# Layer 3 attention: where the first two score products of the next group and the value projections stand on TensorE

## The reference, cut to what matters

```
x = x + L3_xattn(layernorm(x), ctx_1024, mask, W_Q, b_Q, W_K, b_K, W_V, b_V, W_O, b_O)

def L3_xattn(q_input, kv_input, key_padding_mask, ...):      # 16 heads of 8
    q, k, v = q_input @ W_Q + b_Q, kv_input @ W_K + b_K, kv_input @ W_V + b_V
    sim  = einsum('bhqd,bhkd->bhqk', q, k) / sqrt(8)
    sim  = where(mask, neg_inf, sim)
    attn = softmax(sim, axis=-1)
    out  = einsum('bhqk,bhkd->bhqd', attn, v)
    return out @ W_O + b_O
```

## Time and profile before

| | |
|---|---|
| median of 3 runs | 1711.19 us (1710.92 to 1711.9) |
| the profiled execution | 1711.91 us, its span 1709.8 us |
| PE / DVE / ACT busy | 1485.5 / 1249.9 / 841.4 us |
| granted TensorE clock, mean | 0.941 |
| layer 3 attention, first score product to last values product | about 1149 to 1557 us of the span |

### The profile page before, as it was taken

How to read it: one execution, slowest core, us unless ns; L and a number is a source line. 1 busy time by engine, 2 the same in 40 slices (tenths; PEclk the granted TensorE clock), 3 DMA queues, 4 the chain that set the end, 5 groups by cost and what they waited for, 6 DMA issues and landing times. The chain is left out here.

```text
span 1709.8 us, 39665 instructions
## 1 busy us (share of the span) xinstructions
PE 1485.5 (87%) x15230; PEld 1254.1 (73%) x15230; DVE 1249.9 (73%) x2582; ACT 841.4 (49%) x1265; POOL 332.0 (19%) x447
## 2 busy tenths in 40 slices
PE   3897387447899999999999999859999999996995
PEld 2897255236799999999999998426777777774895
DVE  4312664794888888888888886548888888884688
ACT  1342133233666666666666664325656656652432
POOL 0110000001333333333333330030111111100320
PEclk9899699668999999999999999979999999998998
DMA  1455067100211111111111100045455456441010
GB/s 36 112 171 122 20 162 167 37 1 6 67 37 37 37 36 36 36 42 53 46 39 36 36 0 5 2 106 122 118 129 138 111 123 145 116 89 51 26 37 23
DMA packets 93581, 115.95 MB, mean 68 GB/s; under 512 B 12712, under 2 KB 78808, under 8 KB 93464
## 3 DMA queue, kind: packets, MB, share of 16 engines
q1 hardware_dynamic: 93464, 114.25, 26.2%
HBM read 76.42 MB, written 0.46 MB: 45 GB/s over the span
## 5 line engine op out<-in xcount | busy, mean ns | idle before, releaser
L2365 DVE TENSOR_REDUCE l3att_parts<-PS 112x1 f32<-112x500 f32 x384 | 245.5, 668 | 55.8 <-PE PS L2104 48.1
L1643 ACT CAST l2att_PT<-PS 125x512 fp32r<-125x512 f32 x336 | 175.3, 594 | 221.1 <-PE PS L1582 221.1
L1683 DVE TENSOR_REDUCE l2att_neg<-PS 128x1 f32<-128x1500 f32 x112 | 192.7, 1720 | 77.0 <-PE PS L1575 77.0
L1689 DVE TENSOR_TENSOR l2att_PT<-PS,l2att_PT 125x512 fp32r<-125x512 f32 x336 | 210.1, 681 | 1.5 <-ACT l2att_PT L1643 1.5
L2231 ACT ACTIVATE l3att_P<-PS 125x1344 f32<-125x1344 f32 x128 | 165.3, 1292 | 76.9 <-PE PS L2123 76.9
L1582 PEld LDWEIGHTS PS<-all_ident,l_P 128*125 128x125 f32 x1344 | 163.6, 187 | 14.9 <-DVE l_P L1697 6.3
L1652 ACT ACTIVATE l_P<-PS,l2att_neg 128x1500 f32<-128x1500 f32 x112 | 171.3, 1529 | 3.9 <-DVE l2att_neg L1683 3.9
L1614 PE MATMUL PS<-l2att_PT,l_cc 125*128 125x256 f32 x576 | 170.5, 296 | 0.0
L1582 PE MATMUL PS<-all_ident,l_P 128*125 128x128 f32 x1344 | 165.4, 273 | 4.8 <-DVE l_P L1697 4.8
L2104 PE MATMUL PS<-l3att_KS,l3att_QB 97*112 97x500 f32 x384 | 155.8, 459 | 11.1 <-POOL l3att_QB L2291 4.9
L1616 PE MATMUL PS<-l2att_PT,l_cc 125*128 125x256 f32 x576 | 162.5, 282 | 0.0
(11 more groups left out here) (546 smaller groups left out, 2861.3 us busy)
## 6 DMA issues: line engine op xcount, KB each, us to landing
l3att_KS<-l3att_kh SPq DMA_DIRECT2D x128, 187.5 KB, 4.2
l_cT<-in_ctxT SPq DMA_DIRECT2D x18, 750.0 KB, 6.7
l_c<-in_ctx SPq DMA_DIRECT2D x16, 750.0 KB
l3att_cT<-in_ctxT SPq DMA_DIRECT2D x16, 750.0 KB, 4.4
l3att_KS<-l3att_kl SPq DMA_DIRECT2D x64, 187.5 KB, 4.4
l_QP<-in_ctx SPq DMA_DIRECT2D x10, 672.0 KB
l_QP<-in_ctxT SPq DMA_DIRECT2D x8, 750.0 KB, 7.2
l0f_w<-in_L_ffn_W SPq DMA_DIRECT2D x16, 256.0 KB, 3.0
```

What stands on the lines that cost most here:

```text
L1643: act.copy(PT[:, 4 * g:4 * g + 4, PLACE[u1], 0, :], PS[0:CHUNK, 3 * s1 + g, :].rearrange("k (c r) -> k c r", r=128)).then_inc(hi_in, 1)
L1683: v.tensor_reduce(neg[:, s:s + 1], E, XY_AXES, ALU.max, negate=True).then_inc(top_in, 1)
L1689: v.tensor_tensor(PT[:, 4 * g:4 * g + 4, at, 1, :], PS[0:CHUNK, 3 * s1 + g, :].rearrange("k (c r) -> k c r", r=128), PT[:, 4 * g:4 * g + 4 ...
L2365: v.tensor_reduce(parts[:, u % 2, half, i:i + 1], PS[0:HROWS, PLACES[p], 0:BANK_KEYS], X_AXIS, ALU.max, negate=True).then_inc(top_in, 1)
```

## The change

All the changes are in the order of work inside a step of the layer 3 attention. No instruction is added, removed or changed in shape.

- On TensorE `rows((0, 1))` of group n+1 now stands in step n, after the products with the values and ahead of `turned(1)`. `rows` takes the group's number for that.
- `project_values` moves from between score products 2 and 3 to behind the products with the values. Its wait on `p_in` is now for `powers(0)` of the same step, and the wait for ScalarE's copy of bank 5 moves from `turned(0)` to `turned(1)`.
- On ScalarE `values_out` moves from ahead of `powers(0)` to behind `outputs`.

```diff
--- before.py
+++ after.py
@@ -2078,24 +2078,24 @@
                     late = g == 1 and (known is None or SETS < known < GROUPS)
                     weighs = g == SETS - 1 and live(known, 2 * SETS - 1, GROUPS)
 
-                    def rows(places):
-
-                        s = u // SETS
+                    def rows(n, places):
+
+                        s, g = n // SETS % 2, n % SETS
                         for p in places:
                             half, i = p // BANKS, p % BANKS
                             if p == 0:
                                 pe.wait_ge(ks_in[s][g], n // UNROLL * 48 + 48)
                                 if g == 0:
                                     pe.wait_ge(mask_in[s], n // UNROLL * 16 + 16)
-                                if known == 0:
+                                if n == 0:
                                     pe.wait_ge(ones_in, 64)
                                 pe.wait_ge(qb_in, n + 1)
-                                if known != 0:
+                                if n > 0:
                                     pe.wait_ge(top_in, 6 * n - 1)
                             elif 2 <= p <= 4:
                                 pe.wait_ge(top_in, 6 * n + p - 1)
                             elif p == 5:
-                                if known is None or known >= 1:
+                                if n >= 1:
                                     pe.wait_ge(top_in, 6 * n)
                                 if g < BANKS and more:
                                     pe.wait_ge(kl_in, b * BANKS + BANKS + g + 1)
@@ -2114,7 +2114,7 @@
                         if known is None or known - 1 + part > 0:
                             pe.wait_ge(p_in, 2 * n - 2 + part)
                         for k in range(PART):
-                            if k == 4 and part == 0:
+                            if k == 4 and part == 1:
                                 if late:
                                     pe.wait_ge(vh_in, b * BANKS + BANKS)
                                 if g >= 2 and more:
@@ -2151,8 +2151,8 @@
                         mm.then_inc(o_ps, 1)
 
                     now, then, before = live(known, 0, GROUPS), live(known, 1, GROUPS), live(known, 2, GROUPS)
-                    if now:
-                        rows((0, 1))
+                    if n == 0:
+                        rows(0, (0, 1))
                     if then:
                         maxima()
                     if g < BANKS and more:
@@ -2165,22 +2165,22 @@
                                   OC[:, bass.ds((n - SETS) // SETS, 1), :, :].rearrange("p b g q -> p (b g q)"),
                                   start=True, stop=True).then_inc(den_ps, 1)
                     if now:
-                        rows((2,))
+                        rows(n, (2, 3))
+                    if then:
+                        turned(0)
+                    if now:
+                        rows(n, (4, 5))
+                    if before:
+                        values()
                     if late or g >= 2 and more:
-                        if known is None or known >= 2:
-                            pe.wait_ge(p_in, 2 * n - 2)
+                        if n >= 1:
+                            pe.wait_ge(p_in, 2 * n - 1)
                         if late:
                             project_values(pe, u // SETS, 2, 5)
                         else:
                             project_values(pe, 1 - u // SETS, g - 2, 5)
-                    if now:
-                        rows((3,))
-                    if then:
-                        turned(0)
-                    if now:
-                        rows((4, 5))
-                    if before:
-                        values()
+                    if n + 1 < GROUPS:
+                        rows(n + 1, (0, 1))
                     if then:
                         turned(1)
 
@@ -2248,14 +2248,14 @@
                             act.wait_ge(inv_in, (n - SETS) // SETS * 2)
                         act.copy(den[:, :, :].rearrange("p g q -> p (g q)"), PS[:, SIDE, 0:SET_ROWS]
                                  ).then_inc(den_in, 1)
+                    if live(known, 1, GROUPS):
+                        powers(0)
+                    if live(known, 2, GROUPS):
+                        outputs()
                     if g >= 2 and more:
                         values_out(act, b + 1, 1 - u // SETS, g - 2, 5)
                     if g == 1 and (known is None or SETS < known < GROUPS):
                         values_out(act, b, u // SETS, 2, 5)
-                    if live(known, 1, GROUPS):
-                        powers(0)
-                    if live(known, 2, GROUPS):
-                        outputs()
                     if live(known, 1, GROUPS):
                         powers(1)
 
```

## The result

The changed kernel takes 1725.74 us in the median of 4 runs (1723.33 to 1729.49), the kernel before in the same comparison 1711.06 us (4 runs, 1710.34 to 1711.9). The ratio is 1.0081, with a 95% interval of 1.0067 to 1.0095: slower by 0.8%. The profiled execution took 1725.39 us with a span of 1723.3 us, 13.5 us more than the span before.

A forecast was written before the change was run, and what follows sets the result against it. Bound: TensorE near its limit, in a ring of waits between three engines. +9.5 us for 14 batch entries, -0.7 twice in the last, +0.4 in the first: +8.5, 1720.4 profiled, median 1719.7; range 1705 to 1728, own 1714 to 1725.

The forecast's parts named there:

- the signs named for it: TensorE stalls for kl (0.4 to 0.5 us, three steps of four), waits for the exponential in all four, no copy wait.
- The kl ring: Step with g of 2: kh behind the exponential, then kl ending at 2.85, then product 5 at 3.00; 0.48 us lost.
- the term of +0.48: Step with g of 2: product 5 could start at 2.52 but waits for kl until 3.00 us.
- The copy's wait: Inside the transposed scores: the old 0.28 us wait for ScalarE's copy of the value projection goes.
- VectorE's bound in the step with g of 0: The next pair needs maximum 4's bank, so it starts at 4.83 and the step takes 5.93 us.
- the pair and the last half: Step with g of 2: next group's pair 5.65 to 6.10, then second half of transposed scores 0.65, ending at 6.75 us.
- The restart that I put on the value projection: A slow first product after the values, 0.10 us, making the value projection 0.97; charged in three steps.
- The rival with free restarts: Restarts cost nothing where work simply queues: +2.9 us, 1714.1 us, no measurable change; chance 0.10.
- the last batch entry: No keys or kl: two steps of 5.23 against 5.57 give -0.7 us, the last step, lacking the pair, another -0.7.
- kl is no limit: Rival: kh and kl done by 2.37, steps 1 to 3 at 6.20: 24.53 per batch entry, 1702.8 us; chance 0.12.
- VectorE alone sets the pace: Rival: VectorE's idle time is filled, 22.5 us per batch entry, 36 us less, 1675 us; chance 0.03.
- both unknown costs at their bad ends: Rival: kh after a gap (+6 us) and transposed scores with a restart (+5.6), up to 1731 us; chance 0.12.

The follow-up runs named there:

- after_kl_free: Changed kernel with product 5 waiting only for kh and kl computed from kh, so the result is incomplete: 1714.27 us, 1.0015 of the kernel before.
- after_values_first: Changed kernel, complete, with score product 5 moved behind the products with the values: 1711.41 us, 0.9998 of the kernel before.
- after_short_exp: Changed kernel with each step's second exponential reading two of its three banks, from the third step on: 1713.92 us, 1.0014 of the kernel before.
- proj_alone: Kernel before with only the value projections and their copies moved behind the products with values, pair unmoved: 1752.51 us, 1.0233 of the kernel before.
- gap4: Kernel before with score product 4 issued inside the transposed scores, before their fifth product: 1701.02 us, 0.9932 of the kernel before.
- gap4_g0: Kernel before with score product 4 inside the transposed scores and the early pair only for groups with g of 0: 1701.66 us, 0.9941.
- g0_early: Kernel before with the next group's pair early only where that group has g of 0: 1712.05 us, 1.0001 of the kernel before.
- pair_alone: Kernel before with only score products 0 and 1 of the next group moved early, value projections unmoved: 1728.56 us, 1.0092 of the kernel before.

## Why the prediction was right, and where it was short

The direction and the mechanism were right, and so were the signs named for it, with one reservation: the wait for the exponential is marked in one step of four, and in the others only the starts show it. In size the forecast was well short: 8.6 us were forecast (1711.06 to 1719.7) and 14.7 measured (1725.7). That is inside the range of 1705 to 1728, which runs from a gain of 6 us to a loss of 17, but outside the forecast's own (1714 to 1725) by 0.7 us. Of the 6 us that are missing 2.7 are in batch entries 1 to 14, where the mechanism acts.

- **The kl ring** was placed to 0.03 us. After the transposes of the step with g of 2, forecast and measured: kh 1.39 and 1.39, kl 2.12 and 2.09, product 5 3.00 and 2.98, values 3.38 and 3.36, value projection 4.68 and 4.65. after_kl_free and after_values_first take the wait away in two ways and both give 6.33 us: the term of +0.48 measures 0.46.
- **What holds kl** was less sure than it looked. The forecast let kh, behind the exponential, come last (2.12 against 2.06 by VectorE's own order). after_short_exp shows that VectorE's order gives 2.08 or 2.09 by itself. The lag from maximum 2 to kl is 0.60 or 0.61, where 0.59 was taken. So the wait would have come without the exponential too, and that kh's chain gave the right number is in part luck.
- **The copy's wait is gone**, as said, and proj_alone shows why: it is the pair that covers it.
- **VectorE's bound in the step with g of 0** holds (pair 4.83 and 4.85 us after the transposes), and after_kl_free keeps it. Its consequence for the next step was too large: the next group's first maximum comes at 1313.31, which is 5.69 us after the transposes and not 5.86. So VectorE's lateness doesn't reach kl in the step with g of 1 (it starts 2.09 us after the transposes, 1313.65 to 1315.74, as in the step with g of 2, where 2.23 was forecast), and that step is 6.79 and not 6.86.
- **Mis-sized: from the exponential to the transposed scores.** The forecast took 0.05 from a value projection behind the exponential; measured are 0.14 (1301.48 + 1.29 = 1302.77, next product at 1302.91). In the step with g of 3, which waits for nothing else, that makes +0.09 of its +0.14.
- **Mis-sized: the pair and the last half.** The pair behind values or value projection takes 0.53 to 0.54 (1325.98 to 1326.52), not 0.45; the last half 0.70 (1326.52 to 1327.22), not 0.65, in the three steps with a value projection; against it the value projection takes 0.90 from start to start and not 0.97. Together that is +0.06 or +0.07 in each of these three steps, and +0.09 in the step with g of 0. The 0.45 was read from a pair that two transposes follow; the row of a pair with other work behind it has 0.54 (1309.76 to 1310.30) and was the nearer one. The restart that I put on the value projection stands on what follows it; no run isolates why. The rival with free restarts is out, since such costs show in two places.
- Per batch entry the four steps are off by +0.09, -0.07, +0.04 and +0.14, 0.20 us, which in 14 is the missing 2.7 us.
- **Mis-sized: batch entry 0**, +0.4 forecast, +2.2 measured. The granted clock over it was 0.78, against 0.87 before. after_short_exp, in which the first steps have the changed kernel's order, took 26.46 us there at 0.88, so about 0.6 of the 2.2 is the order's price and the rest goes with the lower clock, which this order does not force.
- **Right by luck: the last batch entry**, -1.4 forecast, -1.3 measured. Its four steps together give only -0.7 (5.58 to 5.40, 6.27 to 6.32, 5.56 to 5.41 and 5.41 to 4.96), because the mis-sized terms above count here too. The rest is the clock: the last products with values took 2.31 us before (from 1554.69, at a granted clock of 0.58) and 1.37 after (from 1569.42, at 1.00).
- The remaining 1.5 us (0.8 before the attention of layer 3, which the change doesn't touch, less 0.3 behind it, and a median that stands 0.35 above the profiled execution and not 0.7 below) is no effect of the change that I can show.
- Rivals: "kl is no limit" forecast 24.53 us per batch entry and no wait; there are 42 waits. Even with kl free the steps are 6.33 and not 6.20, by the same mis-sized terms that make the step with g of 3 6.34, so that kernel takes 25.04 and gains nothing on before. "VectorE alone sets the pace" is out: its idle time grew (0.89 to 1.02, and 0.52 more). Of "both unknown costs at their bad ends", kh overlaps as forecast (0.10), and the transposed scores paid half of their restart (0.05) in three steps.

## What to carry to other kernels

On an engine that issues in order, work that stands between a producer's input and its consumer is cover, and moving it opens the wait it hid; write the new order down with starts and look for each consumer whose distance to its producer has shrunk, as kl's did when the 1.1 us of projection between them went. Where a trace shows one short wait, first look for a single instruction that depends on nothing there: one product in the 0.28 us wait gained 0.7%, and the new order around it cost 0.8%. And two chains may end within 0.1 us of each other at the same instruction: shortening one (after_short_exp) shows nothing there, but putting the consumer later (after_values_first) serves both. Last, a stretch that comes out as forecast can do so by two errors, as the last batch entry did; look at its steps and at the granted clock before counting it as understood.

## What the runs showed of the hardware that I had not expected

- At the start of this layer's attention the granted clock is at its lower level (1.2 GHz) for part of batch entry 0, and how long differs: over that stretch it was 0.87 before, 0.78 after, 0.81 in gap4 and 0.67 in gap4_g0, in 25.85, 28.01, 25.33 and 28.96 us. The order differs too, but with the pair's place of gap4_g0 g0_early took 25.94 us at 0.87, so that about 3 us of one execution go with the clock, more than some edits here.
- The lag from the end of an exponential to the first product behind it was 0.05 us for the value projection (and again in pair_alone, 1302.92 to 1302.97) and 0.14 for the transposed scores. Why they differ is open.
- The profiled execution of after_kl_free has five pauses of TensorE, four in the middle of products with values and one in a value projection, which no semaphore explains (marked as issue), and a lower clock after the second (0.84 over 1514.10 to 1525.00). Their sum, and the second of them:

```profile
PE PS L2148 <- issue: 6.5, 4, 2.7
...
1521.05 0.28 PE L2148 MATMUL PS<-l3att_P,l3att_VS 125*9 125x56 f32 x7 [2.71 <-issue]
1521.26 2.07 PE L2047 MATMUL PS<-l3att_wv,l3att_cT 128*125 128x128 f32 x8
```

They end at 1511.80, 1521.05, 1530.88, 1538.43 and 1545.42 and take 1.08, 2.71, 1.74, 1.00 and 0.78 us, and the value projection at 1521.26 takes 2.07 us and not 1.14. No other profile here has such a pause in this attention, and the cause stays open. Together with the lower clock they make that one span some 10 us longer. Three more of the kernel's twelve runs are as long; whether they have such pauses is not known.
